# Moving one of a step's weight pieces on GpSimd from the fifth stage to the eighth, and forming the ranks in five products

## The reference

```python
def reference(x, ctx_1024, g_xattn, g_ffn, wq, wk, wv, wo, w_router, wg, wu, wd, g1, g2):
    x = x + tanh(g_xattn[0]) * cross_attention(layernorm(x), ctx_1024, ctx_1024)   # 16 heads of 16
    return x + tanh(g_ffn[0]) * layer(layernorm(x))

def layer(x):
    h = x + causal_attention(rmsnorm(x, g1), wq, wk, wv, wo)      # 16 heads, rotary positions
    return h + moe(rmsnorm(h, g2), w_router, wg, wu, wd)

def moe(x):                                                       # x: 4096 tokens
    probs = softmax(x @ w_router)
    topw, topi = top_k(probs, 2)                                  # two experts of a token
    topw = topw / sum(topw)
    combine = sum(one_hot(topi, 8) * topw[..., None])
    eo = (silu(x @ wg) * (x @ wu)) @ wd                           # hidden size 704
    return sum over experts of eo * combine
```

## Time and profile before

| | |
|---|---|
| Median of 3 executions | 1544.46 us (1543.71 to 1545.99) |
| Profiled execution, its own time | 1545.92 us |
| Its span in the profile | 1544.1 us |
| Mean granted PE clock | 0.984 of full speed |
| PE busy | 1426.3 us, 92% of the span |
| DVE busy | 1006.0 us, 65% |
| POOL busy | 881.0 us, 57% |
| ACT busy | 779.5 us, 50% |
| Attention steps | the first some 1000 us of the span |
| Expert stage | the rest |

### The profile page before, as it was taken

The page is one execution under the profiler, slowest core; times in us unless marked ns, Lnnn a source line. Parts: engine busy times, 40 slices in busy tenths (PEclk is TensorE's granted clock), DMA queues, the critical chain, the costliest instruction groups (busy, mean ns, idle before and its releaser), DMA issues.

```text
span 1544.1 us, 30418 instructions
## 1 busy us (share of the span) xinstructions
PE 1426.3 (92%) x9013; PEld 856.7 (55%) x9013; DVE 1006.0 (65%) x2351; ACT 779.5 (50%) x1783; POOL 881.0 (57%) x1147
## 2 busy tenths in 40 slices
PE   3999999999999998999999998878899999999997
PEld 1332334444444444444444545457788888888886
DVE  5888767757766765865864755626665656656564
ACT  1576665665665674565666555543233333333332
POOL 7585776974976977787779687445321222222222
PEclk9899999999999998999999999999999999999999
DMA  7756365474574564555473545383354355255220
GB/s 200 193 169 182 97 204 177 147 221 127 176 218 149 169 198 158 174 171 189 141 219 110 175 145 172 130 308 95 64 150 115 79 150 154 43 150 152 39 41 11
DMA packets 116514, 230.12 MB, mean 149 GB/s; under 512 B 20101, under 2 KB 82949, under 8 KB 114310
## 3 DMA queue, kind: packets, MB, share of 16 engines
q1 hardware_dynamic: 81394, 150.29, 31.9%
q0 software_dynamic: 26032, 69.82, 16.5%
q10 hardware_dynamic: 8932, 8.07, 2.0%
HBM read 135.10 MB, written 93.14 MB: 148 GB/s over the span
## 4 chain that ended last, share of the span: by engine, by line
PE 70%; DVE 9%; POOL 9%; issue 5%; ACT 3%; DMA 2%; SPq 1%; another core or an unknown queue 0%; POOLq 0%; DVEq 0%; ACTq 0%
PE pv_ps L1124 10%; PE max_ps L1086 9%; PE max_ps L779 9%; PE key_ps L779 9%; PE key_ps L1103 8%; PE pv_ps L813 6%; DVE neg L1409 4%; PE aux L1172 3%; PE aux L1163 3%; PE pv_ps L815 3%; PE turn_ps L800 2%; PE aux L1156 2%; ACT probs L1295 2%; POOL w_parts L1751 1%; PE key_ps L1106 1%
## 5 line engine op out<-in xcount | busy, mean ns | idle before, releaser
L1409 DVE TENSOR_REDUCE neg<-max_ps 128x1 f32<-128x512 f32 (+3 forms) x864 | 542.3, 665 | 275.3 <-PE max_ps L1089 173.4
L1295 ACT ACTIVATE probs<-key_ps 128x512 f32<-128x512 f32 (+3 forms) x1024 | 499.3, 519 | 370.2 <-PE key_ps L1106 172.5
L1086 PE MATMUL max_ps<-k_stack,q_stack 96*128 96x512 bf16 (+3 forms) x1024 | 354.7, 350 | 32.8 <-DVE neg L1409 18.8
L1103 PE MATMUL key_ps<-q_stack,k_stack 99*128 99x512 bf16 (+3 forms) x1024 | 349.9, 343 | 21.9 <-ACT probs L1295 14.3
L612 POOL DMA_INDIRECT out<-part,whose x71 | 109.8, 1546 | 349.6 <-DVE part L664 277.0
L1086 PEld LDWEIGHTS max_ps<-k_stack,q_stack 96*128 96x128 bf16 x1024 | 100.8, 99 | 222.3 <-DVE neg L1409 124.7
L1103 PEld LDWEIGHTS key_ps<-q_stack,k_stack 99*128 99x128 bf16 x1024 | 100.6, 98 | 120.5 <-ACT probs L1295 56.6
L813 PE MATMUL pv_ps<-weights,hidden_t 128*128 (+1 forms) x426 | 160.0, 413 | 1.4 <-DVE hidden_t L689 1.4
L779 PE MATMUL max_ps<-weights,rows_t 128*128 (+2 forms) x642 | 154.1, 385 | 0.0
L779 PE MATMUL key_ps<-weights,rows_t 128*128 (+2 forms) x636 | 151.1, 382 | 1.1 <-issue 1.1
L1124 PE MATMUL pv_ps<-probs,v_cross 128*32 128x512 f32 (+3 forms) x1024 | 132.1, 587 | 3.4 <-ACT out_t L1365 2.1
(11 more groups left out here) (240 smaller groups left out, 2237.4 us busy)
## 6 DMA issues: line engine op xcount, KB each, us to landing
w_split<-w_parts POOLq DMA_DIRECT2D x32, 704.0 KB, 5.4
weights<-w_split SPq DMA_DIRECT2D x8, 2816.0 KB
weights<-w_split SPq DMA_DIRECT2D x8, 1280.0 KB
w_split<-w_parts POOLq DMA_DIRECT2D x16, 512.0 KB, 4.1
kept_sb<-kept SPq DMA_DIRECT2D x16, 512.0 KB
rows<-rows_in ACTq DMA_DIRECT2D x61, 129.0 KB
parts_cross_k<-parts_k SPq DMA_DIRECT2D x48, 128.0 KB
parts_cross_q<-parts_q SPq DMA_DIRECT2D x48, 128.0 KB
```

Of the source, the lines that this page charges most:

```text
L1086: r = mm(ps[:, 0:keys], q_stack[g][0:KROWS, hd, qt * P:(qt + 1) * P], k_stack[g][0:KROWS, hd, 0:keys], start=True, stop=not own)
L1103: r = mm(ps[:, q0:S], k_stack[g][0:KROWS + NEGROWS, hd, kt * P:(kt + 1) * P], q_stack[g][0:KROWS + NEGROWS, hd, q0:S], start=True, stop=no ...
L1295: act.activation(probs[:, kt % 2, hd, q0:S], key_ps[j % 2][:, q0:S], ACT.Exp).then_inc(m["exp_done"], 1)
L1409: v.tensor_reduce(neg[:, g % 2, hd - place_:hd + 1, qt], scores, op=ALU.max, axis=AX.X, negate=True).then_inc(m["max_red"], many)
```

## The change

It has two parts. In steps 1 to 4 the fifth stage takes two weight pieces rather than three, and the eighth takes one rather than none; as the pieces are numbered through, those of the sixth and seventh stage change their widths with it. In every step the pieces of the eighth stage all stand ahead of the maxima's split, where the last one stood behind it. That touches steps -1, 0 and 5 too, which have pieces there by their own rows. And the ranks are made in five products over several tiles' columns at once, rather than 14 over eight columns each; `hot_b` gets a fifth block of zeros for that.

```diff
@@ pieces_in
-    count = lambda n: PIECES_IN_STEP.get(n // 8, (0, 0, 0, 2, 3, 2, 1, 0))[n % 8]
+    count = lambda n: PIECES_IN_STEP.get(n // 8, (0, 0, 0, 2, 2, 2, 1, 1))[n % 8]
@@ flamingo_block
-            hot_b = s1("hot_b", QT, E, dt=BF16)
+            hot_b = s1("hot_b", QT + 1, E, dt=BF16)
@@ extra, on PE
-                        for t in range(QT + 1):
-                            for s_ in range(min(t + 1, QT)):
-                                r = mm(aux[:, t * E:(t + 1) * E], before_b if s_ == t else ones_b, hot_b[:, s_, :],
-                                       start=(s_ == 0), stop=(s_ == min(t, QT - 1)))
+                        flat = lambda tiles: hot_b[:, 0:tiles, :].rearrange("p t e -> p (t e)")
+                        mm(aux[:, 0:(QT + 1) * E], before_b, flat(QT + 1), start=True, stop=False)
+                        for far in range(1, QT + 1):
+                            r = mm(aux[:, far * E:(QT + 1) * E], ones_b, flat(QT + 1 - far), start=False, stop=far == QT)
@@ on DVE, at its start
+                v.memset(hot_b[:, QT:QT + 1, :], 0.0)
@@ choose, on DVE
-                        v.tensor_tensor(hot_b[:, :, :], hot[:, 0, :, :], hot[:, 1, :, :], ALU.add).then_inc(m["hot_r"], 1)
+                        v.tensor_tensor(hot_b[:, 0:QT, :], hot[:, 0, :, :], hot[:, 1, :, :], ALU.add).then_inc(m["hot_r"], 1)
@@ body, on POOL
                         ng = Step(step.i + 1).neg_of(0) if s == 7 else step.neg_of(s + 1)
-                        for n in pieces_in(now)[:-1]:
+                        first = pieces_in(now) if s == 7 else pieces_in(now)[:-1]
+                        for n in first:
                             split_piece(n)
@@ body, on POOL
-                        for n in pieces_in(now)[-1:]:
+                        for n in pieces_in(now)[len(first):]:
                             split_piece(n)
```

## The result

The changed kernel takes 1535.65 us (median of 7 executions, 1532.74 to 1539.71) against 1544.46 (7 beside it, 1543.13 to 1548.84). The ratio is 0.9948, 95% interval 0.9937 to 0.9959, so 8.0 us less by the ratio, 6.3 to 9.7 by its interval, and 8.8 by the medians. The forecast was 12. Its profiled execution took 1535.19 us with a span of 1533.4.

The account below looks back on a forecast made before the run. PE, busy 92% of the span, was taken to bound the kernel. Waits 5.99, clock 2.56, step 1's opening 1.25 and 1.56, and ranks 1.5 summed to 12.9 us, giving 1532.5 us, range 1527.5 to 1540.

Parts of the forecast that it names:

- The waits: PE's fifth-stage waits for POOL's split in steps 1 to 3 go, 5.99 us; ACT's before step 1, 1.25 us.
- The eighth stage's split: In steps 1 to 4 the added piece fits POOL's idle time, 0.79 us left; cost nothing. Late-split rival: 0.03.
- The opening of step 1: Becomes like step 2's as ACT's wait for `xn` goes: 1.25 us, and 1.56 if the clock stays up.
- The ranks: Five products instead of 14 on PE at eight sequences, taken at 0.19 us each: 1.5 us, between 0 and 1.8.
- the extra memset and the wider `hot_b` cost nothing: The ranks' added zero block costs 0 us, since DVE waits for its first input anyhow.
- The clock: PE's clock falls behind step 3's fifth-stage wait, 2.56 us, and at step 1's opening, 1.56 us, go.
- step 3's fall: Lower clock behind PE's 3.18 us fifth-stage wait in step 3, said to go with that wait: 2.56 us.
- VectorE: Rival: POOL's piece slows DVE in the eighth stage, at worst 10.9 us, 1543.5; chance 0.03. Forecast: nothing measurable.
- the clock's falls come back elsewhere: Rival: other falls answer those at 277 and 585 us; only waits and ranks count, 8.8 us, 1536.5; chance 0.23.

Follow-up runs that it names:

- e2: Kernel before with only the eighth stage's order changed, all its pieces ahead of the maxima's split; ratio 0.9995 to the kernel before.
- e3: Kernel before with only the new count row in steps 1 to 4, the eighth stage's piece behind the split; ratio 1.0019 to the kernel before.
- e5: Kernel before with the new count row in step 3 alone, the eighth stage's piece behind the split; ratio 0.9980 to the kernel before.
- e6: Changed kernel with three pieces ahead of the eighth stage's split in steps 1 to 4; ratio 0.9984 to the kernel before.
- e7: Changed kernel with four pieces ahead of the eighth stage's split in steps 1 to 4; ratio 1.0077 to the kernel before.
- e1: Kernel before with only the ranks changed, five products instead of 14, old table and order; ratio 1.0002 to the kernel before.
- e12: Changed kernel with 128 more waits on PE at its start, which lengthen PE's program; ratio 0.9941 to the kernel before.
- e11: Changed kernel with SP's store and load of `kept_sb` in step 6 issued a place earlier; ratio 0.9941 to the kernel before.
- e10: Kernel before with only the wider `hot_b` and its memset, ranks still 14 products; ratio 1.0008 to the kernel before.
- e4: Kernel before with both piece edits, table and order, ranks still in 14 products; ratio 0.9930 to the kernel before.
- e8: Changed kernel with only the piece counts of steps 5 and 6 changed; ratio 0.9942 to the kernel before.
- e9: Changed kernel with the edits of both e8 and e11; ratio 0.9922 to the kernel before.

## Why the prediction was right, and what it had wrong

**The waits** (5.99 + 1.25 us): right, to 0.02 us in each stretch, and shown one by one by e2, e3 and e5.

**The eighth stage's split**: right. 0.79 us in hand in steps 2 to 4 as worked out, and e6 and e7 pass the margin, by little and by much. The opening of step 1 depends on the order, by e3.

**The ranks** (1.5 us): the five cost their lower bound, 5 x 0.024 = 0.12 us, so 0.22 us saved for each sequence, 1.8 in all. What the step "the extra memset and the wider `hot_b` cost nothing" left out is that a shorter program moves the loads of its code. By the stretch between the last two turns this costs 4.5 us in e1 and 4.8 in the changed kernel, more than the ranks bring. Of the 4.8 us PE's busy time takes 2.65 (16.31 against 13.66, at a clock of 0.84), the longer wait the rest. These are rows of single executions. The times don't bear out the whole of it: e1 should then be at 1.0017, e12 and e11 at 0.992 or less, and they came out at 1.0002, 0.9941 and 0.9941.

**The clock** (2.56 + 1.56 = 4.12 us): too large, and the step that failed is the one that tied step 3's fall to its wait. With the same wait the stretch behind it came out between 15.71 and 19.61 us. From the last turn of step 0 to the last of step 4, the kernels with both waits and the opening's (before, e1, e10) take 491.7 us in the mean, those with the changed pieces, two to a stage (the changed kernel, e4, e8, e9, e11, e12), 482.5. Of the 9.2 us the ranks explain 0.4 (four sequences, five kernels of six against one of three), the waits 7.2. That leaves 1.6 us where 4.1 stood for the clock. It is rough, as the means are those of three and six executions, and it is not the clock alone. The lower level lasts 11.4 us in the mean of the three and 4.0 in that of the six; at 0.4 to 0.5 us of PE's time for each of these (1.25 to 1.56 us for 3.4) that is some 3 us, so about 1.4 us was given back in another way. The rows show one place: in step 2, in the stretch ahead of the eighth stage's, PE stands for 1.1 to 1.2 us ahead of a score product in e3, e4, e8, e9, e11 and e12, so that the stretch there takes 16.6 to 16.8 us, against 15.4 to 15.7 in the kernels with the old row in that step. The row of e4:

```profile
479.02 0.28 PE L1103 MATMUL key_ps<-q_stack,k_stack 99*128 99x256 bf16 x1 [1.18 <-issue]
```

The changed kernel's profiled execution has no such wait (15.3 us) and not one fall in these steps; it is a lucky one, not what the change gives. What PE waits for there the profile doesn't say.

**VectorE** was said to be unaffected. In the eighth stage of steps 2 to 4 it is busy for 13.77 us beside two pieces, against 13.50 in the earlier trace rows, and for 14.16 to 14.21 in e4, whose stretches there are 14.87 us; they are 14.0 in the changed kernel and 13.7 to 14.2 in the kernels with old pieces. So this rival had something in it after all, between nothing and 1 us in a step, which the row with one piece didn't show. Three small instructions of DVE tell the cases apart; here what POOL issues and copies in e4's step 2 then, the last of the three in e4, and the same in the kernel before:

```profile
497.69 0.77 POOL L1754 DMA_DIRECT2D w_split<-w_parts  x1
498.37 0.53 POOL L1750 TENSOR_SCALAR w_parts<-w_in 128x256 fp32r<-128x256 f32 x1
...
498.49 0.45 DVE L1514 TENSOR_SCALAR token<-token 128x4 f32<-128x4 f32 x1
```

```profile
497.52 0.17 DVE L1514 TENSOR_SCALAR token<-token 128x4 f32<-128x4 f32 x1
```

With nothing of POOL's beside them, in the kernel before, the three take 0.17, 0.22 and 0.17 us. In the changed kernel they begin 3.4 us into the stretch, run beside the issue of the first piece's store, and take 0.17, 0.28 and 0.39. In e4 they begin at 3.8 us, run beside that issue and the second piece's copy, and take 0.32, 0.46 and 0.45; e11's step 2 is the same as e4 (14.87 us), with the changed kernel's ranks. So the piece does slow DVE, by how the two happen to fall together; the rest of the 0.9 us is the later beginning, and what makes that was not tried.

**The sum.** 7.2 of waits, 1.6 of clock less what was given back, and 1.8 of ranks make 10.6 us; 4.5 given back at the store leave 6.1. Measured are 8.0, 6.3 to 9.7; with the store's wait alone, 2.1, the sum would be 8.5. That the measured time lies within the forecast's range owes something to luck: the forecast had the waits right, the clock too large, and losses at nothing which partly stood there. The time lies where the rival "the clock's falls come back elsewhere" put it, 1536.5, but by another sum: falls were worth some 3 us and not nothing. Forecast and rival both named the right mechanism for the waits.

What stays open: what decides whether a fall follows a given wait, what PE waits for in step 2, how much of the store's cost a usual execution pays, and what brings the long low stretch of e11 and e9 behind the last turn.

## What to carry to other kernels

A wait of the engine that bounds the kernel can be priced from two like stretches to a few hundredths of a microsecond, and that price holds; the clock's fall behind it, read from one execution, is a draw, so enter it at a part of what the row shows. When an engine's instruction count changes, look at which transfers its code loads now meet, and issue a transfer that the bounding engine waits for earlier than it is needed. The place of a moved piece in its stage counts as much as the stage: the same table was 0.2% slower with the piece behind the split and 0.7% faster with it in front.

## What the hardware showed unexpectedly

A load of PE's code (1.33 MB in 81 packets on the page of the kernel before, so 16 KB) takes one DMA engine for 1.35 us in the middle of a store, and the store lands 1.9 us later (4.95 instead of 3.03 us). The clock stood at its lower level for 0 to 17.1 us, by the profiled execution, in the same 540 us of much the same work, and each 3.4 us of it cost PE 1.2 to 1.6 us. A DVE instruction over four columns took 0.17 us by itself, and 0.45 beside a copy on POOL (e4).
